# A two-layer graph-attention kernel: half of each strip's weights turned as bf16 halves, on TensorE and by DMA

## What is computed

```python
h = maximum(layernorm(x), 0)
q, k, v = h @ Wq.T + bq, h @ Wk.T + bk, h @ Wv.T + bv
scores = where(adj > 0, q @ k.T / sqrt(128), -9e15)
x = x + elu(softmax(scores) @ v)                 # first layer
h2 = maximum(layernorm(x), 0)
g = h2 @ W
e = where(adj > 0, leaky_relu((g @ a[:128])[:, None] + (g @ a[128:])[None, :]), -9e15)
x = x + g + softmax(e) @ h2                      # second layer
```

## Time and profile before

| | us |
|---|---|
| median of 3 runs (lowest, highest) | 815.23 (813.96, 816.91) |
| the profiled execution | 811.28 |
| its span, first to last instruction | 809.5 |
| TensorE busy in the span | 765.8 (95%) |
| VectorE / ScalarE busy | 565.6 (70%) / 568.7 (70%) |
| GpSimd busy | 335.4 (41%) |
| mean granted TensorE clock | 0.98 |

### The profile page before, as it was taken

The page is one execution under the profiler, slowest core; times in us unless marked ns, Lnnn a source line. Parts: engine busy times, 40 slices in busy tenths (PEclk is TensorE's granted clock), DMA queues, the critical chain, the costliest instruction groups (busy, mean ns, idle before and its releaser), DMA issues. The chain is left out here.

```text
span 809.5 us, 17843 instructions
## 1 busy us (share of the span) xinstructions
PE 765.8 (95%) x6229; PEld 658.3 (81%) x6229; DVE 565.6 (70%) x1294; ACT 568.7 (70%) x1159; POOL 335.4 (41%) x326
## 2 busy tenths in 40 slices
PE   4979999999999999999999999686799999999997
PEld 3558888888888888888888888564688888888886
DVE  5847777777777777777777777579765775775582
ACT  6926777767767677676776776676669777977911
POOL 1087557577576675766757662235000000000000
PEclk9979999999999999999999999979799999999999
DMA  8058464563644635546455400090033423333200
GB/s 322 4 203 316 143 224 157 175 216 130 220 168 155 231 132 207 181 145 227 146 194 194 145 37 2 1 204 4 10 81 88 87 62 89 87 81 80 50 10 12
DMA packets 83338, 105.67 MB, mean 131 GB/s; under 512 B 68448, under 2 KB 75104, under 8 KB 79200
## 3 DMA queue, kind: packets, MB, share of 16 engines
q1 hardware_dynamic: 82560, 104.87, 41.0%
q10 hardware_dynamic: 576, 0.26, 0.1%
q0 software_dynamic: 160, 0.00, 0.0%
HBM read 69.47 MB, written 18.87 MB: 109 GB/s over the span
## 5 line engine op out<-in xcount | busy, mean ns | idle before, releaser
L568 ACT ACTIVATE pT_high<-ps_t 128x512 bf16<-128x512 f32 x256 | 151.7, 594 | 125.8 <-PE ps_t L722 125.0
L1259 PE MATMUL ps_x<-v,big 128*128 128x258 bf16 x2048 | 231.6, 274 | 2.3 <-issue 2.3
L1259 PEld LDWEIGHTS ps_x<-v,big 128*128 128x128 fp8e4 x2048 | 198.7, 98 | 32.3 <-issue 2.4
L645 DVE TENSOR_TENSOR pT_low<-ps_t,pT_high 128x512 bf16<-128x512 f32 x256 | 176.3, 690 | 46.7 <-ACT pT_high L568 43.0
L633 DVE CUSTOM_DVE_ANT_0 scores<-ps_s,mask_neg 128x1024 f32<-128x1024 f32 x128 | 156.2, 1221 | 68.3 <-issue 68.2
L732 PE MATMUL ps_acc<-v_parts,pT_high 128*128 128x256 bf16 x1024 | 196.4, 273 | 2.0 <-DVE pT_low L645 1.6
L733 PE MATMUL ps_acc<-v_parts,pT_low 128*128 128x128 bf16 x1024 | 182.7, 219 | 0.0
L562 ACT ACTIVATE scores<-scores,neg_max 128x1024 f32<-128x1024 f32 x128 | 145.8, 1142 | 13.7 <-DVE neg_max L639 13.7
L722 PE MATMUL ps_t<-ident,scores 128*128 128x128 f32 x1024 | 154.3, 273 | 0.5 <-DVE pT_low L645 0.5
L800 ACT ACTIVATE big<-s_block,s_col 128x512 fp8e4<-128x512 f32 x224 | 139.4, 718 | 0.0
L722 PEld LDWEIGHTS ps_t<-ident,scores 128*128 128x128 f32 x1024 | 117.1, 140 | 18.7 <-DVE pT_low L645 0.5
(11 more groups left out here) (134 smaller groups left out, 709.0 us busy)
## 6 DMA issues: line engine op xcount, KB each, us to landing
adj_sb<-in_adj SPq DMA_DIRECT2D x32, 2048.0 KB, 8.0
mask_bytes_dram<-mask_bytes SPq DMA_DIRECT2D x32, 512.0 KB, 8.7
x_sb<-in_x SPq DMA_DIRECT2D x8, 256.0 KB, 6.7
out<-res SPq DMA_DIRECT2D x32, 64.0 KB, 1.5
big<-mask_bytes_dram SPq DMA_TRANSPOSE x32, 4.5
raw_w<-in_L_gnn_Wq ACTq DMA_DIRECT2D x1, 64.0 KB, 3.3
raw_w<-in_L_gnn_Wk ACTq DMA_DIRECT2D x1, 64.0 KB, 3.7
raw_w<-in_L_gnn_Wv ACTq DMA_DIRECT2D x1, 64.0 KB, 4.8
```

Of the source, the lines that this page charges most:

```text
L568: nc.scalar.activation(pT_high[j % 4][:], ps_t[j % 3][:], ACT.Copy).then_inc(pT_ready, 1)
L645: nc.vector.tensor_tensor(pT_low[j % 4][:], ps_t[j % 3][:], pT_high[j % 4][:], ALU.subtract).then_inc(low_ready, 1)
L1259: last = nc.tensor.matmul(ps_x[b % 2][k][:], by_key_tile(m, t)[:, b], v1[k][:, t, :].bitcast(BF16), start=(t == 0), stop=(t == T - 1))
```

## The change

1. Parts 2 and 3 of a strip (keys 2048 to 4095) are turned as before, now as groups 0 to 3 (`turn`, `copy_pT`, `turned_low`).
2. Parts 0 and 1 are turned otherwise. The upper 16 bits of each float32 weight, read as bf16 with a step of two, are turned by eight bf16 transposes per part with a bf16 identity (`turn_high`, L790) into one `ps_t` buffer, and ScalarE copies them, 1024 wide (`copy_hiT`, L613). VectorE subtracts that high half from the weights in SBUF (`low_part`, L698, both inputs in SBUF, 1024 wide) into `low`, and SyncE turns `low` by a DMA from SBUF to SBUF (`turn_low`, L502) into `lowT`.
3. Exponentials go in the order of parts 2, 0, 3, 1, and `times_v` takes groups 4 to 7 before 0 to 3.
4. Adjacency strips are loaded in two halves of 1 MB, with one buffer for each half; the mask bytes and the mask are made by halves too. GpSimd's small gate instructions (`pool_gate`) become semaphore increments.

The diff, cut to its core:

```diff
-            adj_sb = [sb(first, f"adj_sb{i}", [D, N], I32) for i in range(2)]
+            adj_sb = [sb(first, f"adj_sb{i}", [D, N // 2], I32) for i in range(2)]
...
+            EXP_ORDER = (2, 0, 3, 1)
+            PV_ORDER = (4, 5, 6, 7, 0, 1, 2, 3)
+            TURNS = 6
...
+                hiT = [sb(c2, f"hiT{k}", [D, PART], BF16) for k in range(2)]
+                low = [sb(c2, f"low{k}", [D, PART], BF16) for k in range(2)]
+                lowT = [sb(c2, f"lowT{k}", [D, 8, D], BF16) for k in range(2)]
...
+                    def turn_low(c, b, k):
+
+                        s = 4 * c + b
+                        sp.wait_ge(low_done, 2 * s + k + 1)
...
+                            sp.wait_ge(pv_done, 8 * s + 2 * k - 2)
...
+                        sp.dma_start(lowT[k][:], low[k][:], transpose=True).then_inc(lowT_in[k], 16)
...
+                    def period(c, b):
+                        turn_low(c, b, 1)
+                        if has(c, b, 2):
+                            store(*at(c, b, 2))
+                        if has(c, b, 4):
+                            for h in range(2):
+                                load(*at(c, b, 4), h)
+                        if has(c, b, 1):
+                            turn_low(*at(c, b, 1), 0)
...
-                        if not isinstance(s, int):
-
-                            nc.gpsimd.tensor_tensor(pool_gate[:, 1 + b:2 + b], pool_gate[:, 0:1], pool_gate[:, 0:1], ALU.add)
-                        nc.gpsimd.tensor_scalar(mask_bytes[b % 2][:], adj_sb[b % 2][:], 1.0, 0.0, ALU.min, ALU.max).then_inc(bytes_ready, 1)
...
+                        for h in range(2):
+                            pool.wait_ge(adj_in[h], 16 * s + 16)
+                            if not isinstance(s, int):
+                                pool.sem_inc(pool_gate, 1)
+                            nc.gpsimd.tensor_scalar(mask_bytes[b % 2][:, half(h)], adj_sb[h][:], 1.0, 0.0,
+                                                    ALU.min, ALU.max).then_inc(bytes_ready, 1)
...
+                    def copy_hiT(s, k):
+
+                        act.wait_ge(t_done, TURNS * s + 5 + k)
+                        wait(act, pv_done, 8 * (s - 1) + 2 * k + 6)
+                        nc.scalar.activation(hiT[k][:], ps_t[(4 + k) % 3][:].bitcast(BF16), ACT.Copy).then_inc(hiT_ready, 1)
...
+                    def low_part(s, b, k):
+
+                        dve.wait_ge(exp_done, 4 * s + EXP_ORDER.index(k) + 1)
+                        wait(dve, lowT_in[k], 16 * s)
+                        p = scores[b % 2][:, part(k)]
+                        nc.vector.tensor_tensor(low[k][:], p, high_half(p), ALU.subtract).then_inc(low_done, 1)
...
+                    def turn_high(s, b, k):
+
+                        pe.wait_ge(exp_done, 4 * s + EXP_ORDER.index(k) + 1)
+                        pe.wait_ge(pT_low_ready, 4 * s + 2 + k)
+                        out = ps_t[(4 + k) % 3][:].bitcast(BF16)
+                        high = high_half(scores[b % 2][:, part(k)])
+                        for t in range(8):
+                            last = nc.tensor.transpose(out[:, D * t:D * t + D], high[:, D * t:D * t + D], ident_half[:])
+                        last.then_inc(t_done, 1)
...
+                        if i < 4:
+                            pe.wait_ge(pT_low_ready, 4 * s + i + 1)
+                        elif i % 2 == 0:
+                            pe.wait_ge(hiT_ready, 2 * s + j // 2 + 1)
+                            pe.wait_ge(lowT_in[j // 2], 16 * s + 16)
```

More of the change, by code:

```diff
@@ L440, in build, with part, half, has @@
                 ps_a = pb(c2, "ps_acc", [D, 2, D])
-                mask_bytes = [sb(c2, f"mask_bytes{i}", [D, N], U8) for i in range(2)]
                 block = c2.enter_context(nc.Block())
+                def part(k):
+                    return slice(PART * k, PART * k + PART)
+                def half(h):
+                    return slice(N // 2 * h, N // 2 * h + N // 2)
+                def has(c, b, off):
+                    return not isinstance(c, int) or 0 <= 4 * c + b + off < T
+                def at(c, b, off):
+                    return (c + (b + off) // 4, (b + off) % 4)
@@ L506, in make_mask @@
[L506 to L509 removed]
+                            pool.sem_inc(pool_gate, 1)
+                        for h in range(2):
+                            out = mask[b % 2][:, half(h)].rearrange("p (g k w) -> p g k w", w=D, k=2)
+                            src = mask_bytes[b % 2][:, half(h)].rearrange("p (g w k) -> p g k w", w=D, k=2)
+                            nc.gpsimd.tensor_scalar(out, src, -NEG, NEG, ALU.mult, ALU.add).then_inc(mask_ready, 1)
@@ L662, in moments_of, with period @@
                         nc.vector.bn_stats(bn, xs)
-                    add_mask(0, 0, (0, 1, 2, 3))
+                    for k in range(NP):
+                        add_mask(0, 0, k)
                     find_max(0, 0)
-                    add_mask(1, 1, (0, 1))
-                    def period(c, b, ahead):
+                    add_mask(1, 1, 0)
+                    low_part(0, 0, 0)
+                    add_mask(1, 1, 1)
+                    def period(c, b):
                         s, bn = 4 * c + b, (b + 1) % 4
-                        first = isinstance(c, int) and c == 0 and b == 0
-                        if not first:
+                        ahead, ahead2 = has(c, b, 1), has(c, b, 2)
+                        if has(c, b, -1):
@@ L713, in make_scores @@
+                            last = nc.tensor.matmul(o, rest, k_hi[:, col], start=False, stop=True)
                         last.then_inc(s_ready, 1)
-                    def transpose(s, b, j):
-                        if j % 2 == 0:
-                            pe.wait_ge(exp_done, 4 * s + j // 2 + 1)
-                        wait(pe, low_ready, 8 * s + (j - 2 if j >= 3 else (-1, 0, -2)[j]))
-                        for i in range(4):
-                            col = 512 * j + D * i
-                            last = nc.tensor.transpose(ps_t[j % 3][:, D * i:D * i + D], scores[b % 2][:, col:col + D], ident[:])
-                        last.then_inc(t_done, 1)
@@ new lines, in times_v @@
+                    def times_v(s, i):
+                        j = PV_ORDER[i]
+                        if i < 4:
[3 more added lines that the diff above has]
+                            pe.wait_ge(lowT_in[j // 2], 16 * s + 16)
+                        if i == 0:
+                            wait(pe, acc_out, s)
+                        for n in range(4):
+                            t = 4 * j + n
+                            if j >= 4:
+                                high, rest = (m[j - 4][:, D * n:D * n + D] for m in (pT_high, pT_low))
+                            else:
+                                high, rest = hiT[j // 2][:, D * (t % 8):D * (t % 8) + D], lowT[j // 2][:, t % 8, :]
+                            nc.tensor.matmul(ps_a[:], high, v_parts[:, t, :, :], start=(i == 0 and n == 0), stop=False)
+                            last = nc.tensor.matmul(ps_a[:, 0, :], rest, v_parts[:, t, 0, :], start=False,
+                                                    stop=(i == NC - 1 and n == 3))
```

275 lines of the change are left out of this document (134 added, 141 removed).

## The result

| | before | changed |
|---|---|---|
| median of 4 runs each (lowest, highest), us | 815.07 (813.96, 816.91) | 795.14 (790.46, 795.76) |
| the profiled execution, and its span | 811.3, 809.5 | 794.8, 793.0 |
| mean granted TensorE clock | 0.98 | 0.97 |

The ratio is 0.9753, 95% interval 0.9731 to 0.9775: faster by 2.5%, 19.9 us, where 27.2 were forecast. The same kernel again, in the first group of experiments, gave 793.85.

The account below looks back on a forecast made before the run. TensorE, always busy, was taken to bound the first layer's 14.55 us strip period. Per strip 1.76 us go and 0.91 come, 0.85 x 32 = 27.2; 815.2 - 27.2 = 788.0 us, range from 788 - 6 to 806.

Parts of the forecast that it names:

- The prediction's own sign of being wrong: Whole kernel: wrong if the bf16 transposes are priced right and the time still isn't 20 us lower.
- The price of a bf16 transpose: TensorE, first layer: 0.057 us each, sixteen per strip for 0.91, replacing 1.76 of float32 groups; gain 0.85 per strip.
- a pace of 0.083 set by the loads: Rival, TensorE: weight loads set the bf16 transposes' pace, 0.083 us each; gain 13.8, time 801.4; 13%.
- the float32 pace: Rival, TensorE: weights read with a step of two load as slowly as float32; gain 0, time 815.2; 5%.
- ScalarE's tail: ScalarE, end of a strip: copies, exponentials and elu run 1.8 us into the next period, without a stall.
- Slack at V1: TensorE's product step needing the turned remainder VectorE makes after `low1`: tightest place, slack 0.4 us, no stall counted.
- The third rival: First layer: small stalls of 0.2 to 0.5 us as `low1` or the copy is late, about 798; 12%.
- The port: VectorE subtractions with two SBUF inputs wait for GpSimd's running instruction: `low1` 0.4 us, `low0` maybe 1.8; no stall.
- DMA: Transposing DMAs of `low` land after 2.2 to 4.4 us each, with cover of 4 to 5 us: free.
- The start: First strips: half a mask comes earlier, but `lowT0` stands behind three strips' loads; 0, within 2 us either way.
- The end: Last strips of the first layer: no scores to hide ScalarE's late work; within 1.5 us.

Follow-up runs that it names:

- the change again: The changed kernel itself, unedited, measured once more as the mark for the other experiments: 793.85 us, ratio 0.9735 to the kernel before.
- The doubled: Changed kernel with VectorE making the `low1` subtraction a second time, into a spare tile: 826.16 us, ratio 1.0152 to the kernel before.
- swapped `low1`: Changed kernel with two VectorE instructions swapped, the mask of part 2 first, then `low1`: 805.77 us, ratio 0.9894 to the kernel before.
- the quarters: Changed kernel with GpSimd making the mask bytes in four instructions of 1024 elements instead of two of 2048: 795.07 us, ratio 0.9775.
- a third transposing DMA: Changed kernel with one more transposing DMA per strip, of `low1` into a spare tile ahead of the real one: 793.11 us, ratio 0.9741.
- the plain order: Changed kernel with the exponentials in the order of parts 0, 1, 2, 3 again: 792.02 us, ratio 0.9716 to the kernel before.
- the halves alone: Kernel before with only adjacency strips, mask bytes and mask in halves, all weights turned as before: 813.24 us, ratio 0.9991.

## Why the prediction was right, and where it wasn't

The forecast was 788.0, measured 795.1, inside the range; the sign and the mechanism held, and a quarter of the gain was missing. The prediction's own sign of being wrong, that the transposes are priced right "and the time still isn't 20 us lower", is met by a hair: 19.9 us here, with 18.3 to 21.9 by the interval, and 20.5 in the change again. The runs can't decide on it.

- **The price of a bf16 transpose** was right: 0.057, a group of eight in 0.46, the period 13.73 for 13.70. The weights' row reads as the fp8 one of the earlier trace rows did: `L790 PEld` 98 ns. The two rivals on this, a pace of 0.083 set by the loads and the float32 pace, are out. Here the Trainium skill's page TensorE: Matmul & The Clock Gate, section Back-to-back issue gap, with about 81 ns per 128-column matmul in a stream of loads and matmuls, differs from the trace: eight bf16 transposes with eight loads between them take 57 ns each, and the measurement decides.
- **ScalarE's tail** was right: the elu ends 1.7 into the next period (1.8), T0's copy at 2.15 (2.4), a 1024-wide copy takes 1.02 (1.0).
- **Slack at V1** was named as the tightest place, rightly, but mis-sized: `low1` runs from +2.8 to +4.0, T1's remainder ends at +5.8, V1 asks at +6.6; the slack is 0.87, not 0.4. Two sizes did that: `low1` starts 0.3 earlier, as the copy does, and the mask and the remainder each start some 0.08 before the instruction ahead of them has ended. Beside that I had let a wait of 0.4 for GpSimd's add use the slack up. It didn't come, as `low1` starts 0.16 ahead of that add and the add waited for it; that order was a close thing, and the forecast had it the other way round. The doubled and the swapped `low1` show that this slack carries the gain: 32 and 12 us. The third rival, small stalls at V1, put the time at about 798, no further from 795.1 than many runs are from each other, but it isn't what happened: TensorE has no wait between 100 and 480 us.
- **The port.** What I took from the earlier trace rows, that a subtraction with both inputs in SBUF waits for GpSimd's running instruction, is borne out by the quarters and by the swap. The rows alone didn't carry it: L805 in the earlier trace rows has one tile and a scalar column as its inputs, and only one of its eight executions, the one of 0.56, differs from 1.30. What the runs show agrees with the Trainium skill's GPSIMD Engine Reference, section Specifications, on the shared SBUF interfaces. `low0` waits up to 1.4 us (2.58 for 1.21), nobody waits for it, and shortening it gave nothing. I hadn't allowed for GpSimd waiting likewise.
- **DMA**: in the change the cover was enough from the second strip on, as said, and in the stage it held with a third transposing DMA too. The landing was mis-sized: 6.2 us for 256 KB in the median (3.0 to 8.2) where I took 2.2 to 4.4 of the earlier trace rows.
- **The start is the step that failed**: "I put the start at 0, within 2 either way". It cost 5.8 us in the profile, and the forecast had also counted the gain of two strips there. I had named the cause, the transposing DMA behind three strips' loads, and priced it at 2: I took the time of the transfers ahead of it, and not that SyncE stands still at a load which waits for GpSimd's mask bytes, which wait for the load before. TensorE waited 3.3 to 4.7 us for that, and I had put nothing down for the clock, which read 0.50 behind the wait and cost an estimated 2.8 us more. Moving two DMA issues ahead of those loads gave 4.6 us back and the forecast's time, 788.1 to 789.3. That it meets the number is in part luck: from T0 of the first to that of the third strip that kernel still takes 1.9 us more than the kernel before, where the forecast had 1.7 less. It waits 1.8 us there for a mask part (`row_max`) and 1.1 for `lowT`, and its clock reads 0.50 behind the first of these waits, from 62.9 to 66.1 us. The cause of the wait for the mask part wasn't tried apart, nor was the clock.
- **The end** was within its bound: 1.5 us gained there.

## What to carry to other kernels

When TensorE paces a stage, a group of instructions is priced by the distance between starts, and the change gives just that, as long as each engine that feeds TensorE keeps its slack: here 0.87 us at one step carried the gain, and one swap of instructions, with no work added, gave over half of it back. A queue that was free in the steady state wasn't free at the start: there the issues in it wait for waits of others, and the order of the first strips has to be laid out by itself, with the first user's transfer ahead of loads that are needed later. A wait of the engine that paces can cost more than its length, as in these first strips, where TensorE's clock was at its lower level behind it. Busy time of two engines that share a port includes their waits for each other, so it says little about how much work fits in.

## What the runs showed of the hardware

- VectorE's 1024-wide subtraction with both inputs in SBUF takes 1.21 us alone and up to 2.91 beside GpSimd; a GpSimd add of 0.46 takes 1.38 when it starts behind such a subtraction, and two mask halves 5.58 for 3.80 of work. In these rows the one that comes second ends about its own length after the other's end, on both sides.
- The DMA share isn't a sum of fixed costs. With the same transfers in the stage it was 0.80 in the change and 0.72 with the plain order or with the quarters; the median landing of `lowT` was 6.2 us in the change, and 3.8 and 4.1 in those two. By the halves alone (0.54 of 14.55) a transposing DMA of 256 KB is (0.80 x 13.73 - 0.54 x 14.55) / 2 = 1.6 us of all 16 engines in the one and 1.0 in the other, and the third one added 1.8. In the first strips the share reads up to 1.06, so it isn't a fraction of a bound at 1.
- Such a DMA holds SyncE while it is issued: 1.23 us at the least, 4.04 in the first strips, where two of them are issued back to back behind a load half.
- TensorE's granted clock read 0.50 while it worked off what a wait of 3.3 us had held up (75.7 to 82.3 us), and again behind two of the five waits of 2.3 us with `low1` made twice; behind the other three it read 1.00.
